# Attention over 16 images on one core: four exponential tiles instead of two, another table of tasks, and the image loop written out

## The reference

```python
h = jnp.einsum('oc,bcn->bno', wp, xf)            # wp: 1536 x 512, rows normalized
q, k, v = jnp.split(h.reshape(B, N, n_heads, 3 * d_k), 3, axis=-1)
q = pixnorm(q) * scale;  k = pixnorm(k) * scale;  v = pixnorm(v)
attn = jax.nn.softmax(jnp.einsum('bihd,bjhd->bijh', q, k), axis=2)
res = jnp.einsum('bijh,bjhd->bihd', attn, v).reshape(B, N, C)
res = jnp.einsum('oc,bnc->bon', wo, res).reshape(B, C, H, W)
return (a_c * x + b_c * res) / div
```

## Time and profile before

| | |
|---|---|
| median of 3 runs | 3130.0 us (3126.65 to 3157.09) |
| profiled execution, its own time | 3130.55 us |
| its span, first to last instruction | 3128.4 us |
| mean granted clock of TensorE | 0.983 of full |
| TensorE matmul busy | 2989.1 us, 96% of the span |
| VectorE busy | 2596.4 us, 83% |
| ScalarE busy | 2403.5 us, 77% |
| GpSimd busy | 480.7 us, 15% |
| DMA queue of the kernel's transfers | 205.58 MB, 31.2% of the 16 engines' span |

### The profile page before, as it was taken

One profiled execution on the slowest core, in us unless ns is written; L12 is line 12 of the kernel. 1 busy time (PEld: TensorE's weight loads), 2 busy tenths in 40 slices (PEclk: granted clock), 3 DMA queues, 4 the chain that ended last, 5 costly groups with the idle time before them and its releaser, 6 DMA issues.

```text
span 3128.4 us, 90952 instructions
## 1 busy us (share of the span) xinstructions
PE 2989.1 (96%) x36928; PEld 2037.3 (65%) x36928; DVE 2596.4 (83%) x3197; ACT 2403.5 (77%) x2993; POOL 480.7 (15%) x678
## 2 busy tenths in 40 slices
PE   6999999999999999999999999999999999999997
PEld 5676666666666666666666666666676666766664
DVE  5898878978788887888878888788887878878986
ACT  5887877878777777777778778687786877868785
POOL 0211121112111121112111121111211121111210
PEclk9999999999999999999999999999999999999999
DMA  3224324242243322334233342332423224243133
GB/s 99 50 40 81 72 36 106 43 87 61 41 101 55 80 59 50 89 60 85 49 61 77 60 85 49 69 76 53 92 53 77 66 46 102 46 76 72 39 76 92
DMA packets 459647, 212.32 MB, mean 68 GB/s; under 512 B 407952, under 2 KB 407952, under 8 KB 459152
## 3 DMA queue, kind: packets, MB, share of 16 engines
q1 hardware_dynamic: 459152, 205.58, 31.2%
HBM read 71.30 MB, written 33.55 MB: 34 GB/s over the span
## 4 chain that ended last, share of the span: by engine, by line
PE 86%; issue 4%; DMA 3%; DVE 3%; ACT 2%; POOL 1%; SPq 0%; ACTq 0%; DVEq 0%
PE ps_pv L932 24%; PE ps_score L911 21%; PE ps_dense L889 12%; PE ps_dense L893 11%; PE ps_dense L891 10%; PE ps_dense L948 3%; PE ps_dense L950 3%; PE ps_dense L949 3%; DMA out<-x_res 1%; DMA x_res<-in_x 1%; DVE probs L724 1%; ACT e_tile L530 1%; DVE x_res L751 0%; DVE probs L715 0%; ACT x_res L557 0%
## 5 line engine op out<-in xcount | busy, mean ns | idle before, releaser
L530 ACT ACTIVATE e_tile<-ps_score,shift 128x1024 f32<-128x1024 f32 x1024 | 1121.5, 1116 | 461.3 <-PE ps_score L911 337.3
L724 DVE TENSOR_TENSOR probs<-e_tile,probs 128x1024 f16<-128x1024 f32 x1024 | 1248.1, 1231 | 69.6 <-ACT probs L537 59.5
L932 PEld LDWEIGHTS ps_pv<-v_pair,probs 128*128 128x128 f16 x24576 | 785.4, 98 | 157.8 <-issue 134.5
L911 PE MATMUL ps_score<-qkT 64*128 64x512 f16 x6144 | 771.8, 385 | 101.4 <-issue 84.1
L932 PE MATMUL ps_pv<-v_pair,probs 128*128 128x65 f16 (+1 forms) x24576 | 832.6, 194 | 3.6 <-DVE probs L724 2.6
L889 PE MATMUL ps_dense<-wpT_hi,x_hi 128*128 128x512 f32 x1536 | 640.9, 417 | 8.5 <-ACT arena L498 3.5
L893 PE MATMUL ps_dense<-wpT_hi,x_lo 128*128 128x512 f32 x1536 | 603.1, 393 | 0.0
L891 PE MATMUL ps_dense<-wpT_lo,x_hi 128*128 128x512 f32 x1536 | 601.2, 391 | 0.0
L911 PEld LDWEIGHTS ps_score<-qkT 64*128 64x128 f16 x6144 | 262.7, 95 | 459.4 <-issue 191.6
L537 ACT ACTIVATE probs<-e_tile 128x1024 f16<-128x1024 f32 x512 | 541.6, 1058 | 24.4 <-ACT e_tile L530 0.4
L715 DVE CAST probs<-e_tile 128x1024 f16<-128x1024 f32 x512 | 356.8, 697 | 172.3 <-PE ps_pv L932 109.9
(11 more groups left out here) (50 smaller groups left out, 1750.0 us busy)
## 6 DMA issues: line engine op xcount, KB each, us to landing
x_raw<-in_x SPq DMA_DIRECT2D x128, 256.0 KB, 3.2
x_res<-in_x SPq DMA_DIRECT2D x128, 256.0 KB, 3.2
out<-x_res SPq DMA_DIRECT2D x128, 256.0 KB, 2.7
arena<-in_w_proj SPq DMA_DIRECT2D x24, 128.0 KB, 3.1
qkT<-arena SPq DMA_TRANSPOSE x128, 5.5
resT<-res_split SPq DMA_TRANSPOSE x128, 3.4
arena<-in_w_out SPq DMA_DIRECT2D x1, 1024.0 KB, 8.1
```

Of the source, the lines that this page charges most:

```text
L530: act.activation(e_tile[:, t % 2, :, :], ps_score[:, t % 2, :, :], ACT.Exp, bias=shift[:, 0:1], scale=1.0 / (QK_UP * QK_UP)).then_inc(exp_ ...
L724: dve.tensor_tensor(probs_of(b, t, 1), e_tile[:, t % 2, :, :], probs_of(b, t, 0), ALU.subtract).then_inc(probs_low, 1)
L911: mm = pe.matmul(ps_score[:, t % 2, h, :], k[rows, k_part, :], q[rows, :, q_part, :], start=(i == 0), stop=(i == 2))
L932: mm = pe.matmul(ps_pv[:, h, o:o + n], probs_of(b, t, part)[:, h, queries], v[:, cols], start=(j == 0 and it == 0 and part == 0 and cols.s ...
```

## The change

1. `e_tile` has four tiles instead of two (`E_BUFS = 4`). The exponential of tile t waits for the low part of tile t - 4. Every reader indexes by `t % E_BUFS`.
2. All tables of ticks are others, and so is the order of tasks on every engine. `PROJ_BANK` and `OUT_BANK` follow the new order (the banks still alternate). Some tasks of the opening are done in image 0 instead.
3. The `Fori` loop is gone: images 1 to 14 are written out on all engines. All waits are for constants.
4. The program is built with a dynamic DMA scratch of 1024 bytes instead of the default.

The arithmetic, the number of matmuls, of activations, of vector operations and of DMAs are unchanged.

```diff
+E_BUFS = 4
-SCORE_AT = (0, 69, 198, 484, 668, 672, 822, 1116, 1405, 1475, 1486, 1514, 1598, 1925, 2219, 2259, 2393, 2399,
...
+SCORE_AT = (0, 31, 174, 529, 887, 1085, 1330, 1365, 1396, 1477, 1527, 1565, 1862, 2088, 2230, 2265, 2291, 2294,
...
-        e_tile = sb("e_tile", [P, 2, 2, NH], F32)
+        e_tile = sb("e_tile", [P, E_BUFS, 2, NH], F32)
...
             body(0, prev=False)
-            if eng is nc.sync:
-                for b in range(1, B - 1):
-                    body(b)
-            else:
-                with eng.Fori(1, B - 1) as b:
-                    body(b)
+            for b in range(1, B - 1):
+                body(b)
...
                 act.wait_ge(scores_done, SLOTS * b + t + 1)
-                after(act, probs_low, SLOTS * b + t - 1)
-                act.activation(e_tile[:, t % 2, :, :], ps_score[:, t % 2, :, :], ACT.Exp,
+                after(act, probs_low, SLOTS * b + t + 1 - E_BUFS)
+                act.activation(e_tile[:, t % E_BUFS, :, :], ps_score[:, t % 2, :, :], ACT.Exp,
...
-    nc = _bacc.Bacc("TRN2", target_bir_lowering=False, num_devices=1)
+    nc = _bacc.Bacc("TRN2", target_bir_lowering=False, num_devices=1, dynamic_dma_scratch_size=1024)
```

More of the change, by code:

```diff
@@ new lines @@
+ATTEND_AT = (173, 382, 900, 945, 1339, 1345, 1422, 1520, 1539, 1619, 2087, 2089, 2246, 2289, 2293, 2460, 2492,
+    2662, 2887, 2919, 2922, 2979, 2991, 2993, 3392, 3453, 3536, 3548, 3794, 3956, 4107, 4125)
+PROJ_AT = (-1889, -1806, -1800, -1615, -1447, -1218, -1176, -1119, -1107, -722, -638, -390, -113, 30, 169, 181,
+    784, 928, 1270, 1333, 1373, 1484, 1528, 1733)
+SQUARE_AT = (-2343, -2225, -2091, -1965, -1962, -1585, -1460, -1452, -1106, -916, -302, 115, 304, 610, 676,
+    775, 872, 890, 941, 964, 1067, 1081, 1278, 1515)
@@ new lines @@
+COPY_AT = (-2227, -2130, -2089, -1963, -1688, -1572, -1459, -1102, -1096, -539, -4, 118, 385, 686, 757, 787,
+    873, 901, 965, 969, 1088, 1350, 1584, 1685)
+REDUCE_AT = (-2416, -1607, -1437, -1228, -1223, -1213, -1133, -1128, -1021, -50, 105, 217, 311, 312, 313, 386,
+    499, 576, 1012, 1053, 1332, 1334, 1506, 1521)
+SEED_AT = (-1101, 387, 1522)
+NORM_AT = (-1087, 338, 2078)
+SCALE_AT = (-910, -766, -53, -24, 548, 572, 573, 579, 1588, 1633, 1634, 1635)
+HIGH_V_AT = (113, 120, 225, 758, 1868, 1872, 2126, 2127)
@@ new lines @@
+LOW_V_AT = (38, 104, 107, 430, 1670, 1721, 2852, 2966)
+TURN_QK_AT = (1235, 1238, 1698, 1735, 2747, 2938, 3072, 3093)
+HIGH_QK_AT = (-1034, 119, 918, 967, 1046, 1083, 1998, 2128)
+LOW_QK_AT = (-235, 103, 664, 1042, 1086, 1523, 2857, 2872)
+TAKE_AT = (577, 1331, 1530, 1711, 2869, 3185, 4044, 4395)
+TURN_RES_AT = (2735, 2991, 2992, 3185, 5230, 5335, 5337, 5786)
+HIGH_RES_AT = (1042, 1661, 1870, 2135, 3004, 3793, 3829, 4806)
+LOW_RES_AT = (1064, 1654, 1717, 2920, 4041, 4096, 4132, 4544)
+OUT_AT = (5190, 5289, 5459, 5462, 6186, 6290, 6388, 6391)
@@ new lines @@
+ADD_OUT_AT = (4670, 4671, 5063, 5146, 5630, 5727, 5755, 5767)
+FINISH_AT = (5020, 5034, 5346, 5478, 5925, 5943, 6089, 6661)
+LOAD_X_AT = (-2859, -2419, -2380, -1510, -1366, -1363, -1107, -1106)
+HIGH_X_AT = (-3128, -3056, -2857, -2585, -2345, -2342, -2101, -2092)
+LOW_X_AT = (-3053, -3030, -2616, -2583, -2554, -2440, -2380, -2371)
+LOAD_RES_AT = (3127, 5330, 5772, 5790, 6834, 6849, 6887, 7084)
+STORE_AT = (5708, 5771, 6819, 6832, 6855, 6873, 7094, 7450)
+PROJ_BANK = (1, 0, 1, 0, 1, 0, 1, 0, 1, 0, 1, 0, 1, 0, 1, 0, 1, 0, 1, 0, 1, 0, 1, 0)
@@ L149 @@
+OUT_BANK = (1, 0, 1, 0, 1, 0, 1, 0)
 FIRST_SCORE_AT = ()
@@ L180 @@
     -3856, -3840, -3824)
-W_HIGH_AT = (-4024, -4016, -4008, -4000, -3784, -3768, -3760, -3728, -3712, -3704, -3696, -3616, -3600, -3592,
-    -3584, -3560)
+W_HIGH_AT = (-4024, -4016, -4008, -4000, -3784, -3768, -3760, -3728, -3712, -3704, -3696, -3640, -3632, -3624,
+    -3616, -3600)
 W_NORM_AT = (-4080, -3976, -3888)
@@ L191 @@
 X_PIECES = [(ct, half) for half in range(2) for ct in range(CT)]
-FIRST_TICK = -3642
-LAST_TICK = 7460
+FIRST_TICK = -3128
+LAST_TICK = 7450
 def prepare_and_attend(nc, x, w_proj, w_out, out):
@@ L536, in high_probs @@
                 act.wait_ge(exp_done, SLOTS * b + t + 1)
-                act.activation(probs_of(b, t, 0), e_tile[:, t % 2, :, :],
+                act.activation(probs_of(b, t, 0), e_tile[:, t % E_BUFS, :, :],
                                ACT.Copy).then_inc(probs_high_act, 1)
@@ L714, in split_probs_high @@
                 after(dve, pv_done, SLOTS * b + t + 1 - PROB_BUFS)
-                dve.tensor_copy(probs_of(b, t, 0), e_tile[:, t % 2, :, :]).then_inc(probs_high, 1)
+                dve.tensor_copy(probs_of(b, t, 0), e_tile[:, t % E_BUFS, :, :]).then_inc(probs_high, 1)
             def split_probs_low(b, t):
@@ L723, in split_probs_low @@
                     dve.wait_ge(probs_high, len(dve_high) * (UNITS * b + u) + dve_high.index(k) + 1)
-                dve.tensor_tensor(probs_of(b, t, 1), e_tile[:, t % 2, :, :], probs_of(b, t, 0),
+                dve.tensor_tensor(probs_of(b, t, 1), e_tile[:, t % E_BUFS, :, :], probs_of(b, t, 0),
                                   ALU.subtract).then_inc(probs_low, 1)
```

59 lines of the change are left out of this document (14 added, 45 removed), and 18 rows, old and new, of tables (EXP_AT, HIGH_P_AT, LOW_P_AT).

## The result

The changed kernel takes 3014.7 us (median of 3 executions, 3014.4 to 3015.0), the kernel before 3128.5 in the same comparison: a ratio of medians of 0.9636, so 3.6% faster. A fourth execution of the changed kernel took 5852.9 us, at full granted clock and for a reason that no run here shows, and isn't counted. The ratio on record is 0.9616, interval 0.9547 to 0.9684. It is a ratio of means, and one execution of the kernel before, at 3157.1 us where the other three took 3126.7 to 3130.0, raises its mean. I predicted 3027.9, with a range of 3012 to 3062. The direction was right and so was most of the size, but the gain was larger than the sum: 3014.7 lies under the sum's own lower bound of 3016, and 0.9616 of the 3130 that I started from is some 3010 us, just under the whole range.

A forecast was written before the change was run, and what follows sets the result against it. TensorE, busy 2989.1 of 3128.4 us, was taken as the bound. From 3130.55: loop edges -108.65, TensorE order +5.6, other engines' order +1.4, four tiles -1.0, giving 3027.9 us, range 3012 to 3062.

The forecast's parts named there:

- the order of the other engines: VectorE and ScalarE fit their work into an image of 184.35 us; +1.4 us in all, bounds 0 and 2.4 an image.
- The loop's edges: Edges between images 1 to 14: writing out the loop removes 84.1 us of idle time and 24.5 of slow clock, -108.65.
- the gap stays: Rival at the image edges: the idle time was the hand-over between two images, so 3137 us; chance 0.04.
- Nothing else lies beside it: At the loop's edges the lost time is all on PE, as ScalarE and VectorE stand still too; part of -108.65 us.
- Straight code costs nothing: Images 1 to 14 written out: straight code has no cost of its own, taken as 0 us.
- The rival that ends slower: Straight code of images 1 to 14 is fetched too late, 0.47 us a packet, sum above 3162 us; chance 0.04.
- Order on TensorE: Three split runs of projections an image cost 0.4 us an image, bounds 0 and 0.6; +5.6 us for 14 images.
- Bank wait: PE's projection waits for VectorE's addition to free a bank: +0.1 us an image, +1.4 us in all.
- VectorE becomes the wait: Rival in steady images: without edge stops VectorE can't catch up, 3060 us, between 3042 and 3090; chance 0.14.
- Four tiles: Two more exponential tiles bring nothing in steady images, only in the tail: -1.0 us, bounds -2.4 and 0.
- Opening: Before the first score: the chain through the first keys' transpose is kept, so 0, at most -0.5 us.
- Better than the sum: Whole kernel: fewer small waits on data and no price for the order, about 3014 us; chance 0.06.

The follow-up runs named there:

- e1: The kernel before with images 1 to 14 written out on all engines and nothing else changed: 3020.41 us, ratio 0.965.
- e5: The kernel before with the loop kept on TensorE alone, the other engines written out: 3126.74 us, ratio 0.9987.
- e6: The kernel before with TensorE written out and the loop kept on ScalarE, VectorE and GpSimd: 3023.34 us, ratio 0.9658.
- e19: e14 with TensorE written out and ScalarE, VectorE and GpSimd looped: 3024.77 us, ratio 0.966.
- e11: The kernel before, looped, with 32 identity transposes (64 instructions) at the start of TensorE's list: 3069.73 us, ratio 0.9804.
- e12: The kernel before, looped, with 64 identity transposes (128 instructions) at the start of TensorE's list: 3079.31 us, ratio 0.9834.
- e10: e2 with TensorE's ticks 30 earlier, so the cut lies behind a score and two attends: 3083.82 us, ratio 0.9849.
- e3: e1 with four exponential tiles and the smaller scratch, in the old order: 3017.39 us, ratio 0.964.
- e4: The changed kernel, but each exponential waits as if there were three tiles: 3113.49 us, ratio 0.995.
- e9: The kernel before, still looped, TensorE's ticks 196 later so its list is cut behind a score and a projection: 3022.93 us, ratio 0.9655.
- e15: e9 with 32 identity transposes (64 instructions) at the start of TensorE's list: 3023.37 us, ratio 0.9658.
- e14: e2 with TensorE's ticks 380 later, the cut behind a score and a projection, one opening projection moved: 3046.14 us, ratio 0.9727.
- e18: e14 with the loop on TensorE alone and the other engines written out: 3045.29 us, ratio 0.9724.
- e17: e14 with 32 identity transposes (64 instructions) at the start of TensorE's list: 3054.38 us, ratio 0.9759.
- e2: The changed kernel with the loop put back on four engines; order, four tiles and scratch kept: 3055.16 us, ratio 0.9756.

## Why the prediction was right or wrong

**The step that failed** is the one on the order of the other engines, with the bound on the tiles. I took +1.4 us for waits on the bank of `ps_dense`, as a race that VectorE might lose, where the new order removes the 4.2 us of such waits that my base held; and I bounded the four tiles at -2.4 us and took -1.0, where the last stretch came out 4.2 us shorter. The rest of the 13.5 us is my base, one trace with a long opening, and not the change. The parts follow.

**The loop's edges: right.** I took 108.65 us. e1, which changes only this, takes 2583.2 us for the 14 images where the profile of before has 2689.55: 106.4. The medians of before and e1 are 109.2 apart. The 84.1 us of gaps went, and 26.5 of busy time with the slow clock; what came back is 4.3 us of waits for the bank, 7.3 in e1 for 3.0 before. "The idle time belongs to the branch, not to the data" is shown by e5 and e6, and the rival "the gap stays" is out. "Nothing else lies beside it" missed those 4.3 us, and for the new order it misses the other engines' jumps, 0.9 us an image in e19.

What I didn't see is that the price belongs to this cut of this list. I read 6.6 us as what a branch costs; it is what this branch costs with two attends ahead of it and its code where it lies. A fetch that is waited for took 3.1 to 3.5 us where it could be seen alone (e11, e12; 2.9 to 3.6 in e10), and the kernel before waited for two. The Trainium skill, in "Runtime: NRT & Kernel Launch", section "Instruction fetch mechanics", says that code is fetched ahead in sequence only and that a taken branch out of the fetched window waits for a fetch; the pieces and the transfers ahead of them agree. Its fetching in blocks agrees too: 328 transfers of 16,384 bytes here.

**Straight code costs nothing: right.** 0.75 us of 2584 are idle. The rival that ends slower is out. (Its threshold is 102.65 us over 287 packets, 0.36 and not 0.37.)

**Order on TensorE, 0.4 us an image, bounds 0 and 0.6: right, and a little small.** TensorE's busy time grew by 7.6 us over the 14 images from e1 to the changed kernel, 0.54 an image, near the 0.6 that the three split runs give. I took 5.6.

**Bank wait, +0.1 us an image: the wrong sign, and the wrong cause.** My base of 184.35 us an image holds 0.3 us of these waits, as image 1 has, so 4.2 in 14 images. None is left: 2580.9 + 7.6 - 4.2 is 2584.3, the chip has 2584.05, and my sum 2587.9. I read the 3.0 us in the earlier trace rows as VectorE being late with its own work and weighed its casts and scales against TensorE's matmuls. But before the additions VectorE was waiting for the residual's load, 57.3 us in e1 and 52.7 in the kernel before:

```profile
DVE x_res L751 <- DMA x_res<-in_x: 52.7, 27, 3.0
```

In the changed kernel it waits there for TensorE's output projection instead, 108.5 us in the 14 images, so it is ahead and the loads are in time. Which of the new tables does that wasn't tested alone. The rival "VectorE becomes the wait" had 0.14; what came of it is the step from 3.0 to 7.3 us in e1, in the old order.

**Four tiles, -1.0 us with a bound of -2.4: undersized, and the bound was wrong.** From the first score of image 15 to the end, before has 195.98 us, e3 192.1 and the changed kernel 191.8, although its first score of image 15 has one attend (1.5 us) fewer ahead of it, which lengthens that stretch. So the tiles alone give some 3.9, and the rest of the new tables 1.9 more. I bounded the gain by VectorE's idle time in 53 us of that stretch. But the wait on the exponentials in the earlier trace rows, 9.1 us in 15 pieces, is spread over all of it, and VectorE, full in one window, can still deliver earlier by starting its run earlier. That row itself would have been the bound; e3 has 4.2 us of it left, the changed kernel 1.8. "No gain in a steady image" holds for the old order (e3). For the new order I wrote only that the tiles "allow the order to run scores further ahead". e4 puts the number to it: without the fourth, 5.2 us an image.

**Opening, 0: wrong, and for the most part not through the change.** The first score of image 1 comes at 242.87 us in the profile of before, at 238.99 in e1, and at 236.79 in the changed kernel. It comes at 239.8 to 240.7 in e9, e11 and e12, which have the old opening and all four loops. So 2.2 to 3.0 of the 6.1 us belong to the one execution that I took my rows from, and e1's 3.9 hold 0.8 to 1.7 more that this doesn't explain. The waits of ScalarE up to 75 us, of before and then of e1, show a load that landed later in that execution:

```profile
ACT res L564 <- DMA arena<-in_w_out: 2.5, 1, 2.5
```
```profile
ACT res L560 <- DMA arena<-in_w_out: 0.4, 1, 0.4
```

In 30 to 40 us the granted clock was 0.83 there and 1.00 in e1. Of the 2.2 us from e1 to the changed kernel, 1.5 are the marker, since the first score of image 1 now has one attend fewer ahead of it. The total of that execution was the median all the same; what else in it ran a little faster isn't settled.

**"Better than the sum", about 3014, with 0.06.** This is the time that came, by half of the mechanism that I gave: the waits on data did shrink. The other half, no price for the order, didn't hold: it cost 7.6 us of TensorE's time and happened to be paid by the waits that went. The 3.9 us of my base weren't in it either, and it counts the waits of the last stretch twice, so the close figure is in part luck.

**What decides the price of TensorE's edge.** The runs by what stands ahead of the branch and by the transfers of code that an edge adds:

| ahead of the branch | two more transfers | three more |
|---|---|---|
| two attends | 3.9 us (e11), 4.5 (e12), 5.5 (e10, new order) | 8.2 (before), 8.1 (e5) |
| a score and a projection | 0.1 (e9, e15) | 2.6 (e14, e18), 3.1 (e17), all new order |

Both matter, and they go the same way in each row and column. An attend and a projection (e2, 34 more transfers in all) cost 3.1. That a score and a projection hide everything in the old order and leave 2.6 us in the new one goes with the third transfer; no run has the new order at that cut with two, so the order itself isn't excluded. e18 excludes that other engines make the pieces. Why the shift of 64 instructions changes the count in e11 and not in e15 or e17 stays open.

## What to carry to other kernels

A gap on "issue" at a loop's edge was paid nearly in full on the engine that bounds the kernel: write that engine's list out, or keep the loop and move its cut, here by one number added to the ticks, which gave 108.5 us where writing out gave 109.2. Count the code's transfers on the page beside it. When an engine is waited for, look for what it waits for itself, here a load. Before a deeper buffer is priced from the busy share of the engine that frees it, read who waits for its content, stretch by stretch; and before an order is called free of a buffer, run it with one buffer fewer. Take the lengths of the opening and the tail from more than one profile where a few microseconds matter.

## What the runs showed that I had not expected

- A TensorE loop of some 18 code transfers a turn can jump back at 0.1 us (e9: 184.6 us an image, as straight code) or at 8.2 us, with the same instructions in the same order.
- 64 more instructions ahead of the loop made the kernel before 60 us faster (3131.3 to 3069.7), by two more code transfers at each edge instead of three, one wait of 3.1 to 3.5 us instead of two, and a clock that fell at fewer of them.
- A stop of 1 to 2.4 us never lowered the granted clock at an edge in e2, e14 and e18, and at two of 13 in e17. After the pieces of 2.9 to 3.6 it fell at some edges (5 in e11, 9 in e10), and after those of 5.9 to 6.7 at all. Away from the edges, it fell after two stops of 2.1 and 2.3 us on `x_res` in e12. In e10 the matmuls of 512 columns went from 0.39 to 0.63 us after a stop of 3.42.
